# Five pieces of order and placement in a scan kernel: who scales the chunks, how diagonals are made, how scores alternate

## The chip, the cores and the metric

The kernel runs on one core of a Trainium2 chip. Its time is device microseconds of one launch; the median of several runs counts. A profile is one further execution, recorded by the hardware profiler. The engines are TensorE (PE: matmuls; PEld is its weight load), VectorE (DVE), ScalarE (ACT), GpSimd (POOL) and SyncE (SP, which here issues all DMAs).

## The reference, cut to what matters

Two layers over x (2 batches, 1024 tokens, 256 features). The first is a selective state-space layer with an MLP, run forward and backward in time; the second is attention with 16 heads of 16 and an MLP of 1024.

```python
def _ssm(h, in_w, xproj_w, dt_bias, A_log, Dskip, out_w):   # fwd, then bwd
    xz = h @ in_w
    xs, z = jnp.split(xz, 2, axis=-1)                       # 512 channels each
    xs = jax.nn.silu(xs)
    proj = xs @ xproj_w
    dt = jax.nn.softplus(proj[..., :D_INNER] + dt_bias)
    Bm = proj[..., D_INNER:D_INNER + D_STATE]               # 64 states
    Cm = proj[..., D_INNER + D_STATE:]
    A = -jnp.exp(A_log)
    def step(hst, ins):
        dt_t, B_t, C_t, x_t = ins
        dA = jnp.exp(dt_t[:, :, None] * A)
        hst = hst * dA + (dt_t * x_t)[:, :, None] * B_t[:, None, :]
        y_t = jnp.einsum('bds,bs->bd', hst, C_t)
        return (hst, y_t)
    ...
    return y * jax.nn.silu(z) @ out_w
# h is a layer norm of x times (1 + scale) plus shift, both from the condition vector
# attention: softmax(q k^T / 4, with a key mask) v, 16 heads; then an MLP
```

## The kernel before

**Units and steps.** Time is cut into two halves of 512 tokens. With 2 directions and 2 batches that makes 8 units, one after the other. A unit has 64 steps, one for each state of the 64. In a step every one of 512 channels (4 tiles f of 128 partitions) is scanned over 512 tokens for this state. The four engines form a pipeline:

- ScalarE makes `decay` = exp(dt x a) for each f (L1091) and, one step ahead, three of four token tiles of dt x x scaled by this state's B (`uT`, L1073).
- TensorE turns them to channels-on-partitions in PSUM (`turn_u`, L1652 and L1655). Of the four token tiles, three are plain transposes (L1655) and one (L1652) is a product with a diagonal matrix `diag` that holds B, which scales and turns at once. It then sums the products of step w - 2 over the states into four PSUM banks (`reduce_state`, L1661).
- VectorE scans (L1319), one instruction for each f.
- GpSimd multiplies the states by the row of C (L789), two f at a time.

Rings tie them: three PSUM banks for `turn_u` (TensorE can be three tiles ahead of the scan), three buffers of decay and uT (ScalarE up to three steps ahead), three of the states.

**Diagonals.** In the first unit ScalarE makes the diagonal tile of every step (L1076, in `scan_input`). For later units the diagonals lie in DRAM: SyncE fills a zeroed array (`fill_diag`, 16 fills for each of two arrays, one fill for each pair of steps of the first unit), stores B onto its diagonal (`store_diag`, 8 stores a unit) and loads two tiles for each pair of steps (`load_diag`). On the same queue it asks for the rows of C for each pair, first in each pair.

**Tiles between the steps.** All other matrix work of the layer is cut into tiles that have a fixed slot among the steps. `TURN[u]` (from `place_turns`, and `turns` for the last unit) says which tile TensorE begins at which step; each step gives it one piece (one matmul over 512 columns, or a group of transposes) after the second f. `act_turns` and `dve_turns` say what ScalarE and VectorE do after the scans of that step or one to six later: evict the tile, centre a chunk, take silu. Layer norm goes by chunks of 512 tokens: `mean` (TensorE), `centre` (VectorE), `square` (ScalarE, into `sq`), `sum` (TensorE), `std` (ScalarE, into `rstd`) and two steps after the sum `scale` (VectorE, L1183 and L1191: times rstd, then times scale plus shift, one tensor_scalar for each of two feature tiles). Inside the scan lie the scales of chunks 2 and 3 of `ln0` in the first unit, and chunks 0 to 2 of `ln1` in the last.

**Attention.** 16 blocks v of 16 m. For each m TensorE makes two scores that are exponentiated (`scores2`, three PSUM banks, freed by ScalarE's exp, L1116) and two first-pass scores of a later head (`scores`, L1712), whose maxima VectorE takes (L1382, four banks). After every second m come the products with v (`weigh_v`, L1739). 84 of the 512 first-pass scores are made before the blocks.

Of the kernel before, what the change touches and what calls it, by code (L numbers as in the profile page):

```python
# [54 lines left out]
SILU_STEP, LAST_SILU_STEP = 24, 18  # L55
# [5 lines left out]
DIAG_STORES = 8  # L61


def build(nc, t):
# [4 lines left out]
    with ctx:  # L69
# [79 lines left out]
        sq = {name: cut(at, 2, C, HALF) for name, (at, _) in NORM_AT.items()}  # L149
# [104 lines left out]
        def turns(u):  # L254

            yT_ = [("yT", u - 1, f) for f in range(NI)]
            zs_ = [("zs", u, c) for c in range(TB)]
            out_ = [("out", u - 1, c) for c in range(C)]
            return yT_ + zs_ + out_ + steps("mean", "ln1", 0, 1, 2) + steps("sum", "ln1", 0, 1, 2)\
                + up("ln1", 0, 0, 8)[::2] + up("ln1", 0, 0, 8)[1::2] + [("down", "ln1", 0, c) for c in range(C)]  # L260

        def place_turns(u):
# [18 lines left out]
            if u == 0:  # L281
                place(zs_[:2] + steps("mean", "ln0", 2, 3) + xs_[:2] + steps("sum", "ln0", 2, 3) + xs_[2:] + zs_[2:], 0)
# [43 lines left out]
        def dve_turns(u, st):  # L326
# [217 lines left out]
        def _(sp):  # L544
# [43 lines left out]

            def fill_diag(k):

                half, part = divmod(k, FILLS)
# [3 lines left out]
                dst = diag_dram[1 - half, part * n:(part + 1) * n].rearrange("n (k t) -> (n k) t", t=2 * P)\  # L595
                    .rearrange("(p r) t -> p r t", p=P)
                sp.dma_start(dst, zeros.unsqueeze(1).to_broadcast([P, n // 2, 2 * P]))                    .then_inc(s[f"diag_zero_{1 - half}"], 16)

            def store_diag(u, part):
# [3 lines left out]
                if u < 3 and part == 0:  # L603
                    sp.wait_ge(s[f"diag_zero_{u % 2}"], 16 * FILLS)
# [4 lines left out]
            def load_diag(p):  # L609

                u, pair = divmod(p, DS // 2)
                if u == 0 or u == UNITS:
                    return
                if pair == 0:
                    sp.wait_ge(s["diag_out"], 16 * DIAG_STORES * u)
                sp.wait_ge(s["u_full"], NI * 2 * (p - DIAG_PAIRS + 1))
                n = p - DS // 2
# [6 lines left out]
            for u in range(UNITS):  # L624
                sp.wait_ge(s["bc_out"], 16 * (u + 1))
                for pair in range(DS // 2):
# [7 lines left out]
                    if u == 0:  # L634
                        fill_diag(pair)
# [112 lines left out]
        def _(pool):  # L748
# [13 lines left out]

            def finish_dt(u, f):
# [11 lines left out]
            for u in range(UNITS):  # L775
                d, b, hi, half = unit(u)
                for st in range(DS):
# [60 lines left out]
        def _(act):  # L838
            def square(name, i):
# [9 lines left out]
                act.activation(sq[name][:, i % 2], src, ACT.Square).then_inc(s["squared"], 1)  # L849
# [215 lines left out]
            def scan_input(w, c):  # L1065
# [9 lines left out]
                elif u == 0:  # L1075
# [52 lines left out]
        def _(dve):  # L1128
# [64 lines left out]
            def copy_rows(u):  # L1193
# [3 lines left out]
                if u:  # L1197
                    dve.wait_ge(s["bc_out"], 16 * u)
                    dve.wait_ge(s["diag_out"], 16 * DIAG_STORES * (u - 1))
# [225 lines left out]
        def _(pe):  # L1425
# [17 lines left out]
            def mean_square(name, i):  # L1443
                pe.wait_ge(s["squared"], CHUNKS * NORMS.index(name) + i + 1)
                dst = take(pe, first["sum", name, i])
                yield from product(dst, [(mean_w[:, :], sq[name][:, i % 2, c]) for c in range(C)])
# [194 lines left out]
            def turn_u(w, f):  # L1641
# [3 lines left out]
                if f == 0:  # L1645
                    pe.wait_ge(s["uT_ready"], TB * (w + 1) - max(0, w + 1 - DS))
                if f == 0 and w % 2 == 0 and w >= DS:
                    pe.wait_ge(s[f"diag_in_{p % 2}"], 16 * ((p - DS // 2) // 2 + 1))
# [67 lines left out]
            def scores2(v, m):  # L1716
# [6 lines left out]
                for jj in range(2):  # L1723
                    j = 2 * pair + jj
                    n = 2 * w + jj
                    if n >= 3:
                        pe.wait_ge(s["probs_ready"], n - 2)
                    pe.matmul(psum[:, n % 3, :], stack[u % STACKS][0:ROWS, 1, j, kt * P:(kt + 1) * P],  # L1728
                              stack[u % STACKS][0:ROWS, 0, j, tok(qh)], start=True, stop=True)\
                      .then_inc(s["s2_full"], 1)  # L1730
# [77 lines left out]
```

## Time and profile before

| | us |
|---|---|
| runs, median (lowest, highest) | 3275.02 (3272.62, 3275.12) |
| the profiled execution's own time | 3272.75 |
| its span, first to last instruction | 3270.9 |
| TensorE busy, share of the span | 3194.7, 98% |
| VectorE busy | 2866.5, 88% |
| ScalarE busy | 2815.5, 86% |
| GpSimd busy | 2327.7, 71% |
| start of the scan's first unit, end of its last | 63.4, 2549.7 |
| attention blocks | 2710.6 to 3079.2 |

The profile's rows name engine, line and tiles. In a timeline a row is: start, length, engine, line, operation, tiles, count, and in brackets the idle time before it and what ended it. Rows of the same line that touch are merged, so that a row's length covers several instructions. `psum` and `arena` are the large tiles in which everything lies.

### The profile page before, as it was taken

What the parts mean: (1) busy time and instruction counts of PE and PEld (TensorE: products, weight loads), DVE (VectorE), ACT (ScalarE), POOL (GpSimd) and SP (SyncE); (2) the same over time, 40 slices, a digit from 0 to 9 for tenths busy, and PEclk for the clock granted to TensorE, in tenths of its full rate; (3) what the DMA queues carried; (4) which work ended last, traced back from release to release, by engine and by line L of the source; (5) the groups of instructions that cost most, each with busy time, mean ns of one, the idle gap of its engine ahead of it and who ended that gap; (6) DMA issues with size and microseconds to landing.
All of it is one profiled execution on the core that took longest, in us unless ns stands there. A gap on an engine that the chain in (4) does not pass through costs nothing.

```text
span 3270.9 us, 59384 instructions
## 1 busy us (share of the span) xinstructions
PE 3194.7 (98%) x22634; PEld 2505.6 (77%) x22634; DVE 2866.5 (88%) x2863; ACT 2815.5 (86%) x4659; POOL 2327.7 (71%) x1113
## 2 busy tenths in 40 slices
PE   8999999999999999999999999999999999999899
PEld 5888898999899998999998999999888542222244
DVE  3999999999999999999999999999999578888121
ACT  6999999999999999999999999999989436777620
POOL 1899999999999999999999999999878220000000
PEclk8999999999999999999999999999999999999999
DMA  3223222212222222222222222222212043422000
GB/s 121 69 84 81 80 72 69 72 67 72 69 73 93 70 70 75 72 69 72 73 73 74 67 72 67 74 68 71 86 57 69 29 102 59 77 34 31 15 7 20
DMA packets 199837, 218.82 MB, mean 67 GB/s; under 512 B 79969, under 2 KB 149601, under 8 KB 199297
## 3 DMA queue, kind: packets, MB, share of 16 engines
q1 hardware_dynamic: 199554, 215.02, 23.1%
q8 instruction: 180, 2.95, 0.4%
q14 instruction: 103, 0.84, 0.1%
HBM read 194.29 MB, written 18.19 MB: 65 GB/s over the span
## 4 chain that ended last, share of the span: by engine, by line
PE 76%; ACT 15%; DVE 6%; issue 3%; DMA 0%; POOL 0%; DVEq 0%; ACTq 0%; SPq 0%
PE psum L1661 21%; PE psum L1429 17%; PE psum L1655 16%; PE psum L1652 12%; ACT arena L1091 6%; ACT arena L1073 5%; PE psum L1739 4%; PE psum L1728 3%; DVE arena L1319 2%; PE psum L1712 2%; DVE row_max L1382 2%; PE psum L1681 1%; ACT arena L1116 1%; ACT arena L1076 0%; ACT arena L920 0%
## 5 line engine op out<-in xcount | busy, mean ns | idle before, releaser
L1319 DVE TENSOR_TENSOR_SCAN arena<-arena,psum 128x512 f32<-128x512 f32 x2048 | 2373.8, 1230 | 58.6 <-PE psum L1655 45.6
L789 POOL TENSOR_TENSOR arena<-arena 128x1024 f32<-128x1024 f32 x1024 | 2225.8, 2185 | 257.1 <-DVE arena L1319 233.5
L1091 ACT ACTIVATE arena<-arena,a_neg 128x512 f32<-128x512 f32 x2048 | 1442.9, 724 | 45.4 <-PE psum L1655 44.9
L1661 PE MATMUL psum<-ident,arena 128*128 128x128 f32 x8192 | 1231.9, 273 | 1.7 <-POOL arena L789 1.7
L1073 ACT ACTIVATE arena<-arena,bT 128x512 f32<-128x512 f32 x1536 | 1110.7, 723 | 0.0
L1655 PE MATMUL psum<-ident,arena 128*128 128x128 f32 x6144 | 1009.8, 273 | 0.0
L1661 PEld LDWEIGHTS psum<-ident,arena 128*128 128x128 f32 x8192 | 962.7, 141 | 2.1 <-POOL arena L789 2.1
L1652 PE MATMUL psum<-arena 128*128 128x128 f32 x4096 | 821.1, 282 | 31.8 <-ACT arena L1073 16.5
L1652 PEld LDWEIGHTS psum<-arena 128*128 128x128 f32 x4096 | 648.3, 191 | 246.6 <-issue 151.9
L1655 PEld LDWEIGHTS psum<-ident,arena 128*128 128x128 f32 x6144 | 744.2, 142 | 0.0
L1429 PE MATMUL psum<-arena 128*128 128x512 f32 (+1 forms) x1440 | 672.0, 587 | 5.2 <-DVE arena L1191 2.9
L1429 PEld LDWEIGHTS psum<-arena 128*128 128x128 f32 x1440 | 248.7, 192 | 172.4 <-issue 163.8
L1116 ACT ACTIVATE arena<-psum 128x512 f32<-128x512 f32 x512 | 267.2, 604 | 108.1 <-PE psum L1728 108.1
L1382 DVE TENSOR_REDUCE row_max<-psum 128x1 f32<-128x512 f32 x512 | 317.0, 682 | 44.8 <-PE psum L1712 44.1
L833 POOL TENSOR_TENSOR arena<-arena 128x512 f32<-128x512 f32 x8 | 10.2, 1274 | 385.5 <-DMA arena<-sums_dram 385.5
L1728 PEld LDWEIGHTS psum<-arena 100*128 100x128 bf16 x512 | 39.3, 97 | 179.1 <-ACT arena L1116 155.4
L1728 PE MATMUL psum<-arena 100*128 100x512 bf16 x512 | 160.4, 386 | 8.6 <-ACT arena L1116 6.6
L1712 PE MATMUL psum<-arena 97*128 97x512 bf16 x512 | 157.8, 386 | 6.6 <-DVE row_max L1382 6.6
L1739 PE MATMUL psum<-arena 128*32 128x512 f32 x1024 | 136.4, 604 | 4.6 <-ACT skip_w L1106 4.5
L1012 ACT ACTIVATE arena<-psum,b_up 128x512 f32<-128x512 f32 x32 | 22.0, 687 | 101.9 <-PE psum L1429 101.9
L1712 PEld LDWEIGHTS psum<-arena 97*128 97x128 bf16 x512 | 50.6, 99 | 67.9 <-DVE row_max L1382 22.3
L1233 DVE SCALAR_TENSOR_TENSOR arena<-psum,b_up,arena 128x512 f32<-128x512 f32 x32 | 24.0, 751 | 75.0 <-PE psum L1429 75.0
(118 smaller groups left out, 871.9 us busy)
## 6 DMA issues: line engine op xcount, KB each, us to landing
arena<-bc_dram SPq DMA_DIRECT2D x256, 512.0 KB, 3.7
arena<-diag_dram SPq DMA_DIRECT2D x224, 128.0 KB, 2.1
arena<-qk_dram SPq DMA_DIRECT2D x96, 128.0 KB
diag_dram<-arena SPq DMA_DIRECT2D x32, 256.0 KB, 4.4
qk_dram<-arena SPq DMA_DIRECT2D x8, 768.0 KB, 3.4
arena<-in_x SPq DMA_DIRECT2D x4, 512.0 KB, 10.5
arena<-skip_w SPq DMA_DIRECT2D x64, 32.0 KB, 2.0
arena<-sums_dram SPq DMA_DIRECT2D x64, 32.0 KB, 1.8
```

The source lines that it names most:

```text
L789: pool.tensor_tensor(out[:, :, way], h_now[:, :, way], c_row, ALU.mult)\
L1073: act.activation(uT[w % AHEAD][:, c - DIAGS], dtxT[:, u % 2, c], ACT.Copy, scale=bT[:, u % 2, c, st:st + 1])\
L1091: act.activation(decay[:, w % AHEAD, f], dt_[:, u % 2, f], ACT.Exp, scale=a_neg[:, d, f, st:st + 1])\
L1116: act.activation(probs[:, w % 4, jj], psum[:, n % 3, :], ACT.Exp)\
L1319: dve.tensor_tensor_scan(hs[:, w % RING, f, rows][:, way], decay[:, w % AHEAD, f, way], psum[:, 4 + n % U_BANKS, way], end_state(w - DS, f ...
L1382: dve.tensor_reduce(row_max[:, j, qt, kh:kh + 1], side_bank("scores", w), axis=AX.X, op=ALU.max)\
L1429: o = pe.matmul(dst, lhsT, rhs, start=k == 0, stop=k == len(pairs) - 1)
L1652: o = pe.matmul(dst[:, c * P:(c + 1) * P], dtxT[:, w // DS % 2, c, f * P:(f + 1) * P], diag[:, p % DIAG_PAIRS, w % 2], start=True, stop=True)
L1655: o = pe.transpose(dst[:, c * P:(c + 1) * P], uT[w % AHEAD][:, c - DIAGS, f * P:(f + 1) * P], ident[:, :])
L1661: return pe.matmul(psum[:, c, f * P:(f + 1) * P], hs[:, w % RING, f, at:at + P], ident[:, :], is_transpose=True, start=False, stop=w % DS ...
L1712: pe.matmul(take_side(pe, "scores", w), stack[u % STACKS][0:PLAIN, 0, j, qt * P:(qt + 1) * P], stack[u % STACKS][0:PLAIN, 1, j, tok(kh)], ...
L1728: pe.matmul(psum[:, n % 3, :], stack[u % STACKS][0:ROWS, 1, j, kt * P:(kt + 1) * P], stack[u % STACKS][0:ROWS, 0, j, tok(qh)], start=True, ...
```

## The change

Chunks inside the scan are scaled by GpSimd instead of VectorE, at the same step (two after the sum). The last unit's tiles stand in another order; its silu comes at step 23 instead of 18, and the squares of its chunks go to another place (that of `xs`, hence a new wait). In the first unit the chunks' means and sums are spread. Diagonals of the first unit's steps 32 to 63 come from DRAM: half of the second array is filled first, two fills for each of the first four pairs, then four stores are made in pairs 4 to 7; the other fills follow. In attention `scores2` makes one score at a time, and a first-pass score follows each.

```diff
-SILU_STEP, LAST_SILU_STEP = 24, 18
+SILU_STEP, LAST_SILU_STEP = 24, 23
...
+ACT_DIAGS = 32
...
-        sq = {name: cut(at, 2, C, HALF) for name, (at, _) in NORM_AT.items()}
+        def sq(name, i):
+            at = R_XS if name == "ln1" and i < CHUNKS - 1 else NORM_AT[name][0]
+            return cut(at + i % 2 * C * HALF, C, HALF)
...
-            return yT_ + zs_ + out_ + steps("mean", "ln1", 0, 1, 2) + steps("sum", "ln1", 0, 1, 2)\
-                + up("ln1", 0, 0, 8)[::2] + up("ln1", 0, 0, 8)[1::2] + [("down", "ln1", 0, c) for c in range(C)]
+            return steps("mean", "ln1", 0) + yT_ + zs_[:1] + steps("sum", "ln1", 0) + zs_[1:2] + steps("mean", "ln1", 1) + zs_[2:]\
+                + steps("sum", "ln1", 1) + out_ + steps("mean", "ln1", 2) + up("ln1", 0, 0, 8)[:4:2] + steps("sum", "ln1", 2)\
+                + up("ln1", 0, 0, 8)[4::2] + up("ln1", 0, 0, 8)[1::2] + [("down", "ln1", 0, c) for c in range(C)]
...
-                place(zs_[:2] + steps("mean", "ln0", 2, 3) + xs_[:2] + steps("sum", "ln0", 2, 3) + xs_[2:] + zs_[2:], 0)
+                place(zs_[:1] + steps("mean", "ln0", 2) + zs_[1:2] + xs_[:1] + steps("sum", "ln0", 2) + steps("mean", "ln0", 3)
+                      + xs_[1:3] + steps("sum", "ln0", 3) + xs_[3:] + zs_[2:], 0)
...
-            back = TURN[u].get(st - 2)
-            if back and back[0] == "sum":
-                todo += steps("scale", *back[1:])
...
+            late_fills = ACT_DIAGS * FILLS // DS
+            FILL_ORDER = [(0, k) for k in range(late_fills, FILLS)] + [(1, k) for k in range(FILLS)] + [(0, k) for k in range(late_fills)]
+            first_stores = DIAG_STORES * (DS - ACT_DIAGS) // DS
+            def fill_at(k):
+                if k < FILLS - late_fills:
+                    return k // 2
+                k -= FILLS - late_fills
+                return 4 + (k * 3 // 4 if k < FILLS else k)
...
-                if u < 3 and part == 0:
-                    sp.wait_ge(s[f"diag_zero_{u % 2}"], 16 * FILLS)
+                if u < 3 and part == (0 if u else DIAG_STORES - first_stores):
+                    sp.wait_ge(s[f"diag_zero_{u % 2}"], 16 * (FILLS if u else FILLS - late_fills))
...
-                if u == 0 or u == UNITS:
+                n = p - ACT_DIAGS // 2
+                if n < 0 or u == UNITS:
                     return
...
                     if u == 0:
-                        fill_diag(pair)
+                        for k in range(2 * FILLS):
+                            if pair == fill_at(k):
+                                fill_diag(k)
+                        if 0 <= pair - FILLS // 4 < first_stores:
+                            store_diag(0, DIAG_STORES - first_stores + pair - FILLS // 4)
...
+            def scale(name, i):
+                k = NORMS.index(name)
+                n = CHUNKS * k + i
+                b, half = chunk(name, i)
+                out = h[:, :, b, tok(half)]
+                pool.wait_ge(s["rstd_ready"], n + 1)
+                pool.tensor_tensor(out, out, rstd[name][:, i].unsqueeze(1).to_broadcast([P, C, HALF]), ALU.mult)\
+                    .then_inc(s["normed"], 1)
+                pool.wait_ge(s["normed"], n + 1)
+                for c in range(C):
+                    pool.tensor_scalar(out[:, c], out[:, c], mods[:, k, C + c, b:b + 1], mods[:, k, c, b:b + 1], ALU.mult, ALU.add)\
+                        .then_inc(s["h_ready"], 1)
...
+                    back = TURN[u].get(st - 2)
+                    if back and back[0] == "sum":
+                        scale(*back[1:])
...
+                if (name, i) == ("ln1", 0):
+                    act.wait_ge(s["reduce_done"], NI * ((UNITS - 1) * DS + 1))
...
-                elif u == 0:
+                elif w < ACT_DIAGS:
                     act.activation(diag[:, w // 2 % DIAG_PAIRS, w % 2], ident[:, :], ACT.Copy, scale=bT[:, 0, c, st:st + 1])\
                        .then_inc(s["uT_ready"], 1)
...
-                if f == 0 and w % 2 == 0 and w >= DS:
-                    pe.wait_ge(s[f"diag_in_{p % 2}"], 16 * ((p - DS // 2) // 2 + 1))
+                if f == 0 and w % 2 == 0 and w >= ACT_DIAGS:
+                    pe.wait_ge(s[f"diag_in_{p % 2}"], 16 * ((p - ACT_DIAGS // 2) // 2 + 1))
...
-            def scores2(v, m):
+            def scores2(v, m, jj):
...
-                    scores2(v, m)
-                    for w in scores_at(v, m):
-                        scores(w)
+                    others = list(scores_at(v, m))
+                    for jj in range(2):
+                        scores2(v, m, jj)
+                        for w in others[jj:jj + 1]:
+                            scores(w)
```

## Rows read from the trace of the kernel before

**Rows 1.** The stretches' table: us, then each engine's busy us, granted clock, DMA.

```profile
core 0: us, PE busy (x) PEld busy (x) DVE busy (x) ACT busy (x) POOL busy (x), PEclk, DMA share, GB/s
231.74:388.25 156.51, 147.22 (x1196) 134.10 (x1195) 146.63 (x129) 156.51 (x275) 148.67 (x73) 1.00 0.29 83
848.75:999.54 150.79, 150.79 (x1219) 137.80 (x1218) 145.74 (x131) 148.92 (x247) 148.16 (x74) 1.00 0.28 83
2221.92:2549.71 327.79, 316.70 (x2459) 283.77 (x2458) 324.81 (x284) 294.67 (x467) 279.89 (x129) 0.98 0.20 67
2404.00:2409.00 5.00, 5.00 (x26) 5.00 (x25) 4.33 (x5) 4.06 (x7) 4.17 (x2) 0.50 0.09 26
```

**Rows 2.** The chain of waits, first unit's second half, shares by line.

```profile
by line: ACT arena L1091 47.4%; ACT arena L1073 36.6%; ACT arena L1076 5.4%; issue 1.7%; ACT arena L888 1.5%; ACT arena L889 1.5%; ACT arena L903 1.3%; ACT arena L899 1.3%; ACT arena L928 1.2%; PE psum L1655 0.8%; PE psum L1661 0.8%; PE psu
```

**Rows 3.** VectorE's timeline in the third unit, and in the last.

```profile
870.18 4.55 DVE L1319 TENSOR_TENSOR_SCAN arena<-arena,psum 128x512 f32<-128x512 f32 x4 [0.25 <-PE psum L1655]
...
943.73 46.75 DVE L1319 TENSOR_TENSOR_SCAN arena<-arena,psum 128x512 f32<-128x512 f32 x42
...
2242.18 52.99 DVE L1319 TENSOR_TENSOR_SCAN arena<-arena,psum 128x512 f32<-128x512 f32 x45
```

**Rows 4.** ScalarE's timeline, step starts in the first unit and the third.

```profile
229.80 0.73 ACT L1091 ACTIVATE arena<-arena,a_neg 128x512 f32<-128x512 f32 x1
...
234.39 0.74 ACT L1091 ACTIVATE arena<-arena,a_neg 128x512 f32<-128x512 f32 x1
...
968.87 1.35 ACT L1091 ACTIVATE arena<-arena,a_neg 128x512 f32<-128x512 f32 x2
...
973.16 1.36 ACT L1091 ACTIVATE arena<-arena,a_neg 128x512 f32<-128x512 f32 x2
```

**Rows 5.** Groups by line, ScalarE in the first unit.

```profile
L1076 ACT ACTIVATE arena<-ident,bT 128x128 f32<-128x128 f32 x62 | 25.7, 415 | 5.9 <-PE psum L1655 5.9
```

**Rows 6.** DMA issues: KB each, median us to landing.

```profile
arena<-diag_dram SPq DMA_DIRECT2D x224, 128.0 KB, 2.1
...
diag_dram<-arena SPq DMA_DIRECT2D x32, 256.0 KB, 4.4
```

**Rows 7.** VectorE's timeline around the last unit's second and third scale.

```profile
2398.28 1.19 DVE L1183 TENSOR_TENSOR arena<-arena 128x1024 f32<-128x1024 f32 x1
2399.50 2.72 DVE L1191 TENSOR_SCALAR arena<-arena,mods 128x512 f32<-128x512 f32 x2
...
2408.88 1.28 DVE L1319 TENSOR_TENSOR_SCAN arena<-arena,psum 128x512 f32<-128x512 f32 x1 [0.64 <-PE psum L1655]
2411.21 2.45 DVE L1319 TENSOR_TENSOR_SCAN arena<-arena,psum 128x512 f32<-128x512 f32 x2 [1.05 <-PE psum L1655]
...
2425.36 3.62 DVE L1319 TENSOR_TENSOR_SCAN arena<-arena,psum 128x512 f32<-128x512 f32 x3 [0.58 <-PE psum L1655]
```

**Rows 8.** Groups by line: busy us, mean ns of one, idle before.

```profile
L766 POOL TENSOR_TENSOR arena<-arena 128x512 f32<-128x512 f32 x28 | 35.8, 1280 | 0.0
...
L1191 DVE TENSOR_SCALAR arena<-arena,cmod 128x512 f32<-128x512 f32 x16 | 8.0, 543 | 0.3
```

**Rows 9.** Timeline of a fed step: GpSimd's product, TensorE that reads it.

```profile
2378.13 2.18 POOL L789 TENSOR_TENSOR arena<-arena 128x1024 f32<-128x1024 f32 x1 [0.17 <-DVE arena L1319]
...
2383.23 0.60 PE L1661 MATMUL psum<-ident,arena 128*128 128x128 f32 x4
...
2383.89 0.49 PE L1655 MATMUL psum<-ident,arena 128*128 128x128 f32 x3
```

**Rows 10.** Timeline of two m in attention.

```profile
2825.13 0.60 PE L1728 MATMUL psum<-arena 100*128 100x512 bf16 x2
...
2825.62 2.07 ACT L1116 ACTIVATE arena<-psum 128x512 f32<-128x512 f32 x4 [0.83 <-PE psum L1728]
...
2826.01 0.65 PE L1728 MATMUL psum<-arena 100*128 100x512 bf16 x2
...
2828.02 0.60 PE L1728 MATMUL psum<-arena 100*128 100x512 bf16 x2
```

More of the change, by code:

```diff
@@ L587, in store_c @@
                 sp.dma_start(bc_dram[u], bc_rows[DS:2 * DS, :]).then_inc(s["bc_out"], 16)
+            late_fills = ACT_DIAGS * FILLS // DS
[6 more added lines that the diff above has]
+                return 4 + (k * 3 // 4 if k < FILLS else k)
             def fill_diag(k):
-                half, part = divmod(k, FILLS)
                 if k == 0:
@@ L594, in fill_diag @@
                 n = DS // FILLS
-                dst = diag_dram[1 - half, part * n:(part + 1) * n].rearrange("n (k t) -> (n k) t", t=2 * P)\
+                which, part = FILL_ORDER[k]
+                dst = diag_dram[which, part * n:(part + 1) * n].rearrange("n (k t) -> (n k) t", t=2 * P)\
                     .rearrange("(p r) t -> p r t", p=P)
-                sp.dma_start(dst, zeros.unsqueeze(1).to_broadcast([P, n // 2, 2 * P]))                    .then_inc(s[f"diag_zero_{1 - half}"], 16)
+                sp.dma_start(dst, zeros.unsqueeze(1).to_broadcast([P, n // 2, 2 * P]))                    .then_inc(s[f"diag_zero_{which}"], 16)
             def store_diag(u, part):
@@ L611, in load_diag @@
                 u, pair = divmod(p, DS // 2)
-                if u == 0 or u == UNITS:
+                n = p - ACT_DIAGS // 2
+                if n < 0 or u == UNITS:
                     return
-                if pair == 0:
-                    sp.wait_ge(s["diag_out"], 16 * DIAG_STORES * u)
+                if n == 0 or pair == 0:
+                    sp.wait_ge(s["diag_out"], 16 * (first_stores + DIAG_STORES * u))
                 sp.wait_ge(s["u_full"], NI * 2 * (p - DIAG_PAIRS + 1))
-                n = p - DS // 2
                 if n >= 2:
@@ L848, in square @@
                 src = (h if name.startswith("ln") else x)[:, :, b, tok(half)]
-                act.activation(sq[name][:, i % 2], src, ACT.Square).then_inc(s["squared"], 1)
+                act.activation(sq(name, i), src, ACT.Square).then_inc(s["squared"], 1)
             def std(name, i):
@@ L1198, in copy_rows @@
                     dve.wait_ge(s["bc_out"], 16 * u)
-                    dve.wait_ge(s["diag_out"], 16 * DIAG_STORES * (u - 1))
+                    dve.wait_ge(s["diag_out"], 16 * DIAG_STORES * (u - 1) + 16 * DIAG_STORES * (DS - ACT_DIAGS) // DS)
                 dve.tensor_copy(bc_rows[:, :], bank(g)).then_inc(s["bc_rows_ready"], 1)
@@ L1445, in mean_square @@
                 dst = take(pe, first["sum", name, i])
-                yield from product(dst, [(mean_w[:, :], sq[name][:, i % 2, c]) for c in range(C)])
+                yield from product(dst, [(mean_w[:, :], sq(name, i)[:, c]) for c in range(C)])
             def h_ready(name, i):
@@ L1722, in scores2 @@
                     pe.wait_ge(s["rows_in"], 16 * PARTS * (u + 1))
[L1723 to L1730, printed above, removed]
+                j = 2 * pair + jj
+                n = 2 * w + jj
+                if n >= 3:
+                    pe.wait_ge(s["probs_ready"], n - 2)
+                pe.matmul(psum[:, n % 3, :], stack[u % STACKS][0:ROWS, 1, j, kt * P:(kt + 1) * P],
+                          stack[u % STACKS][0:ROWS, 0, j, tok(qh)], start=True, stop=True)\
+                  .then_inc(s["s2_full"], 1)
             def weigh_v(v, kt):
```

2 lines of the change are left out of this document (1 added, 1 removed).

## The prediction

> **What bounds the kernel now.** I read the stretches first, then the chain, then single engines. The page's first part has TensorE busy nearly throughout, but that is a mean over stages with different limits. The table of stretches splits the scan [rows 1]. The second half of the first unit (32 steps) takes 156.5 us, with ScalarE busy for all 156.51 of it and TensorE for 147.2. The same half of the third unit has the same scan and the same kinds of tiles, and takes 150.8 us with TensorE busy throughout. So the first unit is held by ScalarE and the later ones by TensorE. The chain of waits says the same of that half: three ScalarE lines, L1091, L1073 and L1076, are 89% of it [rows 2]. L1076 is the instruction that makes a diagonal tile.
>
> The last unit takes 327.8 us with VectorE busy for 324.8 [rows 1]. It is bound by VectorE, which does its 256 scans and all that lies between them.
>
> Three rates are used below. When VectorE is fed, a backward step (4 scans) takes 52.99 x 4 / 45 = 4.71 us, a forward one 46.75 x 4 / 42 = 4.45. When TensorE must add a tile's piece to each step, the step is 4.55 + 0.25 = 4.80 us, the 0.25 being a wait for TensorE; there are 8 such steps on end [rows 3].
>
> **The change part by part.**
>
> *Diagonals of the first unit.* ScalarE starts a step every 234.39 - 229.80 = 4.59 us where it makes one diagonal, and every 973.16 - 968.87 = 4.29 us where it makes none (the second stretch holds no other work) [rows 4]. So one diagonal costs 0.29 to 0.30 us of ScalarE's pace; the 415 ns that its row shows overlap the neighbours [rows 5]. The 32 that go are worth 32 x 0.295 = 9.4 us of ScalarE. What is late next is TensorE at 4.80 per step while tiles are interleaved, and VectorE at 4.45 afterwards. The third unit shows that mix, two output tiles included that the first has not: 150.8. I expect 150, thus 6.5 us won of the 9.4, with 5.7 (156.5 - 150.8) as the low end and 9.4 as the high one. SyncE gets 16 more loads of 128 KB (2.1 us from issue to landing, against some 9.6 us that two steps leave) and 4 small stores, and issues two fills at a time in the first four pairs. The store's wait for the fills stands one pair behind the last of them, and a fill lands 4.4 us after its issue [rows 6]. GpSimd's rows of C are asked for ahead of all these in each pair. I cost it at nothing; a late C row would show as GpSimd waiting for a DMA.
>
> *Chunk scaling from VectorE to GpSimd, twice in the first unit and three times in the last.* On VectorE one takes 1.20 for the product and 2.72 for the two tensor_scalar: 3.9 us until the next scan [rows 7]. The tensor_scalar of the same shape takes 0.54 late in the kernel, where GpSimd is idle [rows 8]; here the first stands until GpSimd's product has ended. Between the second and the third VectorE waited 0.64 + 1.05 us for TensorE, and 0.58 after the third [rows 7]. In that stretch, 2404 to 2409, the granted clock was 0.50, the level of 1.2 GHz, and TensorE had idled during the scaling before [rows 1]. So the last unit loses 3 x 3.9 + 2.3 = 14.0 us.
>
> In the first unit two such holds cost VectorE 7.8 us, but ScalarE, which sets the end there, stood idle for only 5.9 in all, every bit of it waiting for TensorE behind those holds [rows 5]. I take 5.9 for this half; the 2 us that are left are VectorE's new reserve.
>
> What GpSimd pays: it already works 2.18 us per product, two products a step, with idle gaps of some 0.2 [rows 9]. The first operation of a scale is a product of the same size, 2.18. A tensor_scalar of 128x512 is in no row of GpSimd. From below: VectorE's 0.54. From above: a GpSimd sum of two operands of that shape, 1.28 [rows 8], and, further off, one of twice the size, 2.18. I take 1.28, the same engine and shape. A scale is then 2.18 + 2 x 1.28 = 4.7 us (3.3 to 6.5), and the next state product is late by that less 0.2, by 4.5 us.
> The Trainium skill, GPSIMD Engine Reference, section 4.1 (Engine selection), speaks against the change: keep elementwise work on VectorE, GpSimd being about 2x slower with two inputs and near line rate with one. The trace agrees on the first part (2.18 for GpSimd's product of 1024 elements a partition, 1.20 for VectorE's). By that page's best loop (769 ns for 512 elements, section 3.1) a scale would be an estimated 3.7 us and the last unit's loss below would be nil.
>
> Who waits for that: TensorE reads the product that ended at 2380.31 only from 2383.23, 2.9 us later [rows 9]. VectorE then has one scan running and two more tiles ready, between 2.4 and 3.5 us of work at 1.18 a scan, and TensorE's next tile is done 1.15 us after that read (2383.89 + 0.49). That leaves 1.2 to 2.4 more, and I take 1.8. So 4.7 us are free against 4.5. GpSimd catches up by little: two products back to back, with 0.1 between, need 2 x 2.28 of a step's 4.71, 0.15 us a step, and all that VectorE does besides scans (a centring 1.2, an output 0.7). In the new order the last unit's scales come after steps 14, 24 and 40. Between the first two about 3 us are made good, so the second is over by some 1.5 us; before the third all of it is. I book 1.5, with 0 (short form) and 7 (long form) as ends. In the first unit it hides behind the 2 us of reserve and a TensorE that runs less far ahead. VectorE's waits ended by TensorE, TensorE's by GpSimd, is what is late next.
>
> *New order of the last unit's tiles.* The same 21 tiles in the same 56 slots, centrings and outputs at other steps. The silu of the gates goes from step 18 to 23, where ScalarE is again several us ahead. The first square now waits for the first reduction, which is five steps old. With the holds gone TensorE has fewer pauses in which to catch up: up to five more steps at 4.80 in place of 4.71, 0.5 us. Sum of the last unit: 14.0 - 1.5 - 0.5 = 12.0 us.
>
> *Scores one by one.* Per two m TensorE runs 4 second scores, 4 first-pass scores and 8 products with v, in 2828.02 - 2825.13 = 2.89 us. The pair at 2825.13 shows 0.60, that at 2826.01 shows 0.65 [rows 10]: its second matmul waits for the exp that frees its bank. That exp can start only at 2825.62 and needs 0.6. With first-pass scores between, the fourth second score comes at 1.3 us instead of 1.1 and no longer waits. That is 0.05 us per two m, and there are (512 - 84) / 4 = 107 such groups: 4.9 us. VectorE's reduces get their scores evenly, and 4 x 0.6 = 2.4 us of them fit in 2.84. From both sides: a gain of nothing if another wait takes its place, 8 us if it also eases the stalls at the block ends; a loss of 3 if the alternation holds a score back.
>
> **The sum.** 6.5 + 5.9 + 12.0 + 4.9 = 29.3 us off the profiled execution's 3272.75 gives 3243.5. That execution stands 2.3 us below the median of the runs (3275.02), and with the median it is 3245.7. I say 3244.5. I count as no change what lies within 0.2%, 6.5 us, about what a measurement of this kernel can tell.
>
> **The rivals.**
> A. The alternation is worth nothing, since TensorE has no other idle time in the group: 3244.5 + 4.9 = 3249.5. For it: only 0.05 us of waiting in 2.89. Chance 0.12.
> B. GpSimd's tensor_scalar is dear (2.2 us or more). The scale takes 6.5 us, overruns by 1.7, 3.5 and 1.7 in the last unit, and TensorE's pauses bring the half clock back once, 2.3 us as before: 3244.5 + 7.7 = 3252. If it takes 3 us, all five overrun and the moved work gains next to nothing; only the diagonals and the scores stay (11.4): 3275 - 11.4 = 3263.6. Chances 0.12 and 0.06. Against it: the product of two operands costs 1.28.
> C. More is won: a cheap tensor_scalar (no overrun, 1.5), all 9.4 us of ScalarE and the eased block ends (3): 3244.5 - 7.4 = 3237. Chance 0.12.
> D. Slower: GpSimd becomes the bound. A scale of D us costs the scan D - 4.9 each time, less the 2 us of reserve. It eats the whole gain where 5 x (D - 4.9) - 2 exceeds 29.3, at D = 11.2, a tensor_scalar of 4.5 us. At 6 us each (D = 14.2) it is 3244.5 - 1.5 + 44.5 = 3287.5. For it: the form is in no row of GpSimd, and a row of C late on SyncE's queue would add to it. Against: 3.5 times its dearest row of that shape. Chance 0.05.
> E. The first unit stays where it is because something else (GpSimd's products, or TensorE with its half clock early on) sets its pace: 3244.5 + 12.4 = 3257. Chance 0.05.
>
> **The numbers.** My forecast has 0.48 and its own range of 3240 to 3249. The range for 8 in 10 takes in A, C and the first part of B: 3235 to 3256. Faster by over 0.2% (below 3268.5): all but D and part of the dear end of B, 0.92. Within 0.2%: 0.03. Slower: 0.05.
>
> **What would show it.** The first unit's second half near 150 us with ScalarE no longer full, L1076 with 32 instructions, and ScalarE's 5.9 us of waiting gone. The last unit near 316 us, no VectorE row of 2.7 us for the scaling, no stretch at half clock in it, and TensorE waiting for GpSimd's product once, by a few us. A GpSimd tensor_scalar row of 0.8 to 1.3 us. Groups of two m at 2.84 us. Wrong would be: a GpSimd row above 2.2 us, VectorE idle behind TensorE after steps 14, 24 or 40, GpSimd waiting for C, or groups at 2.89 or more.

## The result, and the profile after

The changed kernel takes 3247.64 us (median; 3244.18 to 3249.24) against 3273.82 (3272.40 to 3275.12) of the kernel before on the same chip, a ratio of 0.9917 (95% interval 0.9904 to 0.993). That is 26.2 us less. The forecast was 29.3 by its parts, and 30.5 from the median of 3275.02 to the 3244.5 that it named. A second comparison (the changed kernel beside the combined version, below) gave 0.9913 (0.9898 to 0.9928). The profiled execution took 3246.55 us, its span is 3244.7. VectorE's busy time fell by 21.2 us, ScalarE's by 9.6, and GpSimd's rose by 11.2.

The table of stretches, with the columns of [rows 1], now for the first unit's two halves, the last unit, and a stretch at half clock:

```profile
65.17:230.03 164.86, 158.71 (x1223) 141.86 (x1222) 148.44 (x134) 164.26 (x279) 144.25 (x69) 0.98 0.29 84
230.03:378.05 148.02, 145.08 (x1199) 134.12 (x1198) 144.19 (x130) 145.13 (x240) 145.50 (x72) 1.00 0.30 86
2211.98:2527.69 315.71, 310.79 (x2459) 279.02 (x2458) 313.12 (x275) 294.25 (x466) 287.26 (x137) 1.00 0.21 70
196.20:203.00 6.80, 5.68 (x24) 4.76 (x23) 4.92 (x5) 6.80 (x12) 4.47 (x3) 0.50 0.16 51
```

Set against before, by the same marks (start of the first scan of the stretch to the start of the next stretch's; the last unit to the end of its last scan):

| stretch | before, us | after, us | difference | forecast |
|---|---|---|---|---|
| ahead of the first scan | 63.4 | 65.2 | +1.7 | 0 |
| first unit, steps 0 to 31 | 168.3 | 164.9 | -3.4 | -5.9 |
| first unit, steps 32 to 63 | 156.5 | 148.0 | -8.5 | -6.5 |
| six middle units | 1833.7 | 1833.9 | +0.2 | 0 |
| last unit | 327.7 | 315.7 | -12.1 | -12.0 |
| between scan and attention blocks | 161.0 | 160.9 | -0.1 | 0 |
| attention blocks | 368.6 | 364.1 | -4.5 | -4.9 |
| end | 191.7 | 192.1 | +0.4 | 0 |

Each part came in the stretch where it was expected. In size the last unit and attention agree, while the first unit's halves missed by 2.5 us (too little won) and 2.0 us (more won).

In the first unit's second half ScalarE is no longer full (145.1 of 148.0, against 156.51 of 156.51 in [rows 1]). Two things hold it now, one after the other. For 14 steps TensorE adds a tile's piece to each, and VectorE waits 0.25 us for it in each, 4.81 us a step. From 310.93 on VectorE scans for 67.2 us without a pause:

```profile
294.73 4.55 DVE L1359 TENSOR_TENSOR_SCAN arena<-arena,psum 128x512 f32<-128x512 f32 x4 [0.25 <-PE psum L1695]
...
310.93 67.20 DVE L1359 TENSOR_TENSOR_SCAN arena<-arena,psum 128x512 f32<-128x512 f32 x60 [0.17 <-ACT arena L1131]
```

That is 67.20 x 4 / 60 = 4.48 us a step, near the forecast's 4.45 for a fed VectorE. GpSimd runs without a pause in that time too, and the chain of waits (shares by line, as in [rows 2]) passes through its products; which of the two would have to become faster first, no run shows.

```profile
by line: POOL arena L824 56.9%; PE psum L1701 9.5%; issue 8.8%; PE psum L1695 7.4%; PE psum L1469 5.3%; PE psum L1692 5.0%; POOL arena L808 3.4%; POOL arena L801 2.6%; DVE arena L1359 1.5%; DVEq L1357 0.0%
```

The scaling on GpSimd. First the timeline of one scale in the last unit (start, length, engine, line, ..., count), then the group of its tensor_scalar (busy us, mean ns of one, idle before):

```profile
2288.44 2.38 POOL L791 TENSOR_TENSOR arena<-arena 128x1024 f32<-128x1024 f32 x1
2290.93 1.52 POOL L795 TENSOR_SCALAR arena<-arena,mods 128x512 f32<-128x512 f32 x2
2292.41 6.43 POOL L824 TENSOR_TENSOR arena<-arena 128x1024 f32<-128x1024 f32 x3
```

```profile
L795 POOL TENSOR_SCALAR arena<-arena,mods 128x512 f32<-128x512 f32 x10 | 7.6, 769 | 0.5
```

The scale's product takes 2.38 us, a tensor_scalar 0.77, and from the scale's start to the next state product pass 2292.41 - 2288.44 = 3.97 us. The forecast had 4.7 from two ends, 3.3 and 6.5. Its sentence on the Trainium skill (GPSIMD Engine Reference, section 3.1) had an estimate of 3.7 for the whole and 769 ns for the tensor_scalar; the row of 769 ns agrees.

Two things were not foreseen. The first is in the last unit: TensorE idles before the output tile of step 24. TensorE's row, and ScalarE's around it:

```profile
2332.84 1.10 PE L1469 MATMUL psum<-arena 128*128 128x512 f32 x2 [1.83 <-ACT arena L900]
```

```profile
2323.20 1.28 ACT L960 ACT_TABLE_LOAD   x1
2324.49 1.92 ACT L960 ACTIVATE arena<-arena 128x2048 f32<-128x2048 f32 x1
2326.43 1.28 ACT L1137 ACT_TABLE_LOAD   x1
...
2332.03 0.66 ACT L900 ACTIVATE arena<-psum,eps 128x512 f32<-128x512 f32 x1
```

Silu and two table loads hold ScalarE for 4.5 us at step 23. The sum's eviction (L900) comes behind them and the exponentials and scaled tiles of one more step, at 2332.03. The tiles between the steps share one PSUM bank, so TensorE cannot begin the next tile before, and waits 1.83 us.

The second is in the first unit. TensorE idles behind the silu burst of step 24, and its granted clock falls to 0.50 (1.2 GHz) just after, the stretch 196.2 to 203.0 of the first table. VectorE waited 3.30 us for ScalarE there. The kernel before has the same burst, with one pause of 1.41 us and full clock. The rows are TensorE's before, TensorE's after (two), VectorE's after:

```profile
202.16 0.49 PE L1652 MATMUL psum<-arena 128*128 128x128 f32 x2 [1.41 <-ACT arena L1073]
```

```profile
195.37 0.49 PE L1692 MATMUL psum<-arena 128*128 128x128 f32 x2 [2.29 <-DVE arena L1359]
...
198.03 0.80 PE L1692 MATMUL psum<-arena 128*128 128x128 f32 x2 [1.12 <-ACT arena L1113]
```

```profile
194.10 4.58 DVE L1359 TENSOR_TENSOR_SCAN arena<-arena,psum 128x512 f32<-128x512 f32 x4 [3.30 <-ACT arena L1131]
```

By the starts of the steps' first scans, counted from the unit's first, the changed kernel was 8.1 us ahead of the kernel before when step 24 began, and 3.5 when step 27 began. What VectorE's two holds had cost was won, and over half of it was given back at the burst.

In attention, first- and second-pass scores now alternate every 0.22 us, and the group of two m takes 2813.29 - 2810.45 = 2.84 us against 2.89 [rows 10]:

```profile
2810.45 0.39 PE L1767 MATMUL psum<-arena 100*128 100x512 bf16 x1
2810.67 0.38 PE L1752 MATMUL psum<-arena 97*128 97x512 bf16 x1
...
2813.29 0.39 PE L1767 MATMUL psum<-arena 100*128 100x512 bf16 x1
```

### The profile page after: what moved, and what is told of

It reads as the page before. It is cut to its first block, busy times and chain, and to the rows that moved or that the text cites. A ratio compares the mean times of both kernels' runs of the same rounds, so it can differ in the third digit from the quotient of the medians.

```text
span 3244.7 us, 59428 instructions
## 1 busy us (share of the span) xinstructions
PE 3181.8 (98%) x22634; PEld 2506.4 (77%) x22634; DVE 2845.3 (88%) x2848; ACT 2805.9 (86%) x4627; POOL 2338.9 (72%) x1128
## 4 chain that ended last, share of the span: by engine, by line
PE 72%; ACT 16%; DVE 5%; issue 4%; POOL 3%; DMA 0%; DVEq 0%; ACTq 0%; SPq 0%
PE psum L1701 19%; PE psum L1469 16%; PE psum L1695 14%; PE psum L1692 11%; ACT arena L1131 7%; ACT arena L1113 5%; PE psum L1778 4%; PE psum L1767 3%; DVE arena L1359 3%; POOL arena L824 3%; PE psum L1752 3%; DVE row_max L1422 1%; PE psum L1721 1%; ACT arena L1156 1%; ACT arena L960 0%
## 5 line engine op out<-in xcount | busy, mean ns | idle before, releaser
L1767 PE MATMUL psum<-arena 100*128 100x512 bf16 x512 | 189.9, 384 | 8.6 <-ACT arena L1156 6.6
L1752 PE MATMUL psum<-arena 97*128 97x512 bf16 x512 | 191.9, 387 | 5.3 <-DVE row_max L1422 5.3
L1767 PEld LDWEIGHTS psum<-arena 100*128 100x128 bf16 x512 | 48.2, 97 | 169.1 <-ACT arena L1156 132.5
```

The source lines that it names most:

```text
L1752: pe.matmul(take_side(pe, "scores", w), stack[u % STACKS][0:PLAIN, 0, j, qt * P:(qt + 1) * P], stack[u % STACKS][0:PLAIN, 1, j, tok(kh)], ...
```

## The experiments

All lengths of stretches below are by the marks of the table above, from the profile of each kernel. Except in the comparison marked below, a kernel was timed once. Ahead of the first scan, where nothing differs, these times vary by 4.5 us (last section), so the stretches carry the argument and not the whole times.

**Scaling back on VectorE.**

```diff
 # dve_turns
+            back = TURN[u].get(st - 2)
+            if back and back[0] == "sum":
+                todo += steps("scale", *back[1:])
 # GpSimd's loop
-                    if back and back[0] == "sum":
-                        scale(*back[1:])
```

> The changed kernel, with the scaling of chunks inside the scan back on VectorE at the same steps; the new order, the diagonals and the scores stay. Theory (the holds of VectorE were the loss): the last unit goes from 315.7 us back to 326 to 330 (three holds of 3.9, and up to 2.3 if the pauses of TensorE bring its half clock back), VectorE rows of 2.7 us for the two tensor_scalar reappear five times, the first unit goes from 312.9 to 316 to 319 (ScalarE idles again behind the two holds); in all 14 to 20 us, 3261 to 3267. Rival (the new order of the last unit's tiles won the time): the last unit stays at or below 318 us and the whole within 6 us of 3247.

Measured: 3259.93 us. The last unit takes 326.9 us, 11.2 more than in the changed kernel, which is three holds of 3.9 less a bit; a short spell of half clock came with it.

```profile
2213.47:2540.32 326.85, 313.63 (x2459) 280.59 (x2457) 324.00 (x284) 294.87 (x466) 279.81 (x128) 0.99 0.20 67
```

```profile
L1231 DVE TENSOR_SCALAR arena<-arena,mods 128x512 f32<-128x512 f32 x6 | 8.2, 1401 | 0.1
```

The six tensor_scalar average 1.40 us where they run beside GpSimd's products (0.54 in [rows 8]). With the new order and no move the last unit is only 0.8 us shorter than before (326.9 against 327.7), so the order alone, its silu at step 23 included, won next to nothing. But the move alone does not give 12.1 us either, only 6.8 (the scaling alone, below): it needs the new order, which sets the scales further apart.

The first unit grew by only 1.5 us, less than the 3 to 6 expected, and so the whole is 1 us below the expected range. When step 24 began it was 6.2 us behind the changed kernel, but it made good 4.7 of them at the burst, where its pause was the short one of 1.41 us and the clock stayed full.

**All diagonals by ScalarE.**

```diff
-ACT_DIAGS = 32
+ACT_DIAGS = 64
```

with the fills one for each pair.

> The changed kernel, with all 64 diagonals of the first unit made by ScalarE (the fills then go one for each pair of steps, no loads in the first unit). Theory (ScalarE's 0.295 us for each diagonal set the pace of the second half): its 32 steps go from 148.0 us back to 156 to 158, ScalarE full again, the first half stays within 1 us; in all 8.5 to 9.5 us more, 3255 to 3258. Rival (the move of the scaling, or the clock, made that half quicker): it stays below 151 us.

Measured: 3257.49 us. The second half takes 155.9 us, 7.9 more, with ScalarE at 154.3:

```profile
231.93:387.81 155.88, 146.66 (x1196) 134.04 (x1195) 146.43 (x129) 154.29 (x271) 148.59 (x73) 1.00 0.30 83
```

The theory holds; the size is a hair below its range. 32 diagonals are worth 7.9 us there, not the full 32 x 0.295, since at 148 the half is held by TensorE and then by VectorE and GpSimd. The other 0.6 us of that half's 8.5 is assigned to no part.

**Scores in pairs.**

```diff
-                    others = list(scores_at(v, m))
                     for jj in range(2):
                         scores2(v, m, jj)
-                        for w in others[jj:jj + 1]:
-                            scores(w)
+                    for w in scores_at(v, m):
+                        scores(w)
```

> The changed kernel, with the attention order of before: two second scores, then two first-pass scores. Theory (the fourth second score waited for its bank): a group of two m goes from 2.846 back to 2.89 us and the 16 blocks from 364.1 to 368 to 369 us, in all 4 to 5 us more. Rival (the blocks became shorter by another way, such as the stalls at block ends): the groups' median stays at 2.85 and only the blocks' ends differ.

Measured: 3251.05 us, the blocks 368.8 us against 364.1. A group is 2833.13 - 2830.24 = 2.89 us again, and the second pair of second scores shows 0.65 again:

```profile
2830.24 0.60 PE L1767 MATMUL psum<-arena 100*128 100x512 bf16 x2
...
2831.12 0.65 PE L1767 MATMUL psum<-arena 100*128 100x512 bf16 x2
...
2833.13 0.60 PE L1767 MATMUL psum<-arena 100*128 100x512 bf16 x2
```

**The scaling alone**, put into the kernel before.

> The kernel before, with nothing changed but the scaling moved to GpSimd. A scale there is 2.18 + 2 x 0.77 = 3.7 us, and in this order the last unit has three of them after steps 32, 34 and 36. Theory (2.9 us until TensorE reads a product and 1.8 of tiles ready for VectorE are free, and little is caught up in two steps): the first costs nothing, the second some 2.2 us, the third some 3.3, so the last unit takes 313.7 + 5.5 = 319 us (317 to 321). Rival 1 (only the 2.9 are free): 321 to 323. Rival 2 (GpSimd's lateness is hidden wholly): 314. The first unit: 324.8 less 5.9 of ScalarE's idle time, plus up to 2.4 if the silu burst brings the half clock, 319 to 322. In all 3258 to 3262.

Measured: 3265.80 us; first half 162.2, last unit 320.9. In the last unit the first of the three scales (at 2385.26) cost nothing: VectorE scans on until 2403.31. After the second and the third TensorE waited over 2 us for GpSimd's product, and VectorE behind it:

```profile
67.54:229.73 162.19, 157.32 (x1223) 140.53 (x1222) 148.46 (x134) 161.62 (x276) 144.42 (x69) 0.99 0.24 75
2219.84:2540.71 320.87, 312.83 (x2459) 280.37 (x2458) 313.53 (x275) 294.54 (x467) 287.92 (x137) 0.99 0.20 69
```

```profile
2403.89 0.66 PE L1676 MATMUL psum<-ident,arena 128*128 128x128 f32 x4 [2.36 <-POOL arena L801]
...
2416.35 0.88 PE L1676 MATMUL psum<-ident,arena 128*128 128x128 f32 x4 [2.62 <-POOL arena L801]
```

```profile
2384.12 19.19 DVE L1334 TENSOR_TENSOR_SCAN arena<-arena,psum 128x512 f32<-128x512 f32 x16
...
2418.43 1.28 DVE L1334 TENSOR_TENSOR_SCAN arena<-arena,psum 128x512 f32<-128x512 f32 x1 [2.91 <-PE psum L1670]
2421.20 9.60 DVE L1334 TENSOR_TENSOR_SCAN arena<-arena,psum 128x512 f32<-128x512 f32 x8 [1.50 <-PE psum L1670]
```

The first unit's half is 6.1 us shorter than before, as the forecast's 5.9 had it. In the last unit 7.2 us were lost, 2.7 and 4.5, where 2.2 and 3.3 were expected. The total of 320.9 does not tell the theory (317 to 321) from the rival in which only TensorE's 2.9 us are free (321 to 323). The row of the first scale does: it held GpSimd for 3.96 us, 0.9 more than 2.9 and the gap of 0.2 together, and VectorE did not wait. Of the third scale's 4.5 us the second wait, 1.50, came in a spell of half clock (2416.6 to 2420.1). The whole lies above the expected range, as 4.1 us of it fall ahead of the first scan, where nothing was changed.

**The last unit's silu after step 26.**

```diff
-SILU_STEP, LAST_SILU_STEP = 24, 23
+SILU_STEP, LAST_SILU_STEP = 24, 26
```

> The changed kernel, with the last unit's silu of the gates after step 26 instead of 23. Theory: in the changed kernel TensorE idles 1.83 us at step 24, since its output tile needs the one bank that the sum's tile holds until ScalarE, busy with table loads and silu, evicts it. After step 26 stand output tiles, which VectorE evicts, so that pause goes: step 24 falls from 6.9 to 4.8 us and the last unit from 315.7 to 313.6 (313 to 314.2), 2 us in all. Rival (ScalarE's work as such is late there, and the pause only moves): the last unit stays at 315 to 316.

Measured: 3248.43 us in all, of which 2.7 more than in the changed kernel's profile lie ahead of the first scan. The last unit takes 313.6, 2.1 less, and the whole difference is in step 24 (6.88 us in the changed kernel, 4.80 now):

```profile
2214.71:2528.29 313.58, 310.51 (x2459) 278.91 (x2457) 313.13 (x275) 293.92 (x466) 287.33 (x137) 1.00 0.21 70
```

**Sixteen diagonals by ScalarE.**

```diff
-ACT_DIAGS = 32
+ACT_DIAGS = 16
...
-                    return k // 2
+                    return k // 3
...
-                        if 0 <= pair - FILLS // 4 < first_stores:
-                            store_diag(0, DIAG_STORES - first_stores + pair - FILLS // 4)
+                        for k in range(first_stores):
+                            if pair == FILLS // 4 + k // 2:
+                                store_diag(0, DIAG_STORES - first_stores + k)
```

> The changed kernel, with only 16 of the first unit's diagonals by ScalarE (fills three for each pair, six stores in pairs 4 to 6, loads from pair 8 on). Theory (ScalarE sets the first half as well, and TensorE's pause behind the silu burst brings the half clock): by step 24 ScalarE is 9 x 0.295 = 2.7 us earlier, the pause of 2.3 + 1.1 us shrinks, no half clock near 196 us, and the first half goes from 164.9 to 160 us (159 to 161.5), the second stays at 148. Rival 1 (the half clock stays): 162 to 163. Rival 2 (TensorE or GpSimd bound that half, not ScalarE): 164 to 165. Should SyncE's waits hold back rows of C, GpSimd shows waits for DMA and the half gets longer.

Measured: 3243.72 us. The first half takes 158.9 us, 6.0 less, a little better than 159, and there is no half clock near 196. All but 0.7 us of it is won in steps 24 to 26. Its chain of waits up to the silu burst is TensorE's now:

```profile
67.84:226.69 158.85, 156.55 (x1223) 140.47 (x1222) 148.31 (x133) 158.25 (x261) 144.18 (x69) 0.99 0.33 97
226.69:374.75 148.06, 145.10 (x1199) 134.13 (x1198) 144.25 (x130) 146.14 (x242) 145.45 (x72) 1.00 0.28 79
```

```profile
by line: PE psum L1702 27.2%; PE psum L1696 22.6%; PE psum L1470 16.2%; PE psum L1693 15.9%; DVE arena L1360 7.0%; PE psum L1722 2.9%; issue 2.7%; DVE arena L1204 2.0%; ACT arena L961 1.5%; ACT L1138 1.0%; ACT arena L1132 0.6%; ACT arena L1
```

**A scale nearly twice as long.** After the two tensor_scalar on GpSimd:

```diff
-                        .then_inc(s["h_ready"], 1)
+                        .then_inc(s["again"], 1)
+                scales = (0, 0, 0, 1)[i] if name == "ln0" else 2 + i
+                for r in range(2):
+                    pool.wait_ge(s["again"], C * (2 * scales + r + 1))
+                    for c in range(C):
+                        pool.tensor_scalar(out[:, c], out[:, c], 1.0, 0.0, ALU.mult, ALU.add)\
+                            .then_inc(s["h_ready" if r else "again"], 1)
```

> The changed kernel, with each scale followed by four more tensor_scalar of the same shape on GpSimd (times 1, plus 0), so that it holds GpSimd 2.18 + 6 x 0.77 + waits = 7.0 us instead of 3.7. Theory (2.9 us until TensorE reads, and 1.8 of tiles ready, are free; 3 us caught up in ten steps): the scan loses 2.1, 3.8 and 2.1 us at the last unit's three scales, so the last unit takes 315.7 + 8.0 = 324 us, up to 328 if TensorE's pauses bring the half clock. Rival 1 (only the 2.9 are free): 13.4 us more, 329 or above. Rival 2 (GpSimd is behind anyway and is caught up by what VectorE does besides): below 320. First half of the first unit: 165 to 169.

Measured: 3260.35 us, the last unit 327.3 us, 11.6 more; the first half 165.0. A scale held GpSimd for 6.6 us (the added ones took 0.6 each), not 7.0. The waits of TensorE in the last unit (who waited for whom: us in total, times, longest):

```profile
2213.76:2541.05 327.29, 316.42 (x2459) 282.57 (x2457) 313.46 (x275) 294.68 (x466) 294.94 (x149) 0.98 0.21 67
```

```profile
PE psum L1707 <- POOL arena L830: 6.0, 3, 2.0
```

```profile
2300.76 1.28 DVE L1365 TENSOR_TENSOR_SCAN arena<-arena,psum 128x512 f32<-128x512 f32 x1 [2.01 <-PE psum L1701]
2303.88 2.45 DVE L1365 TENSOR_TENSOR_SCAN arena<-arena,psum 128x512 f32<-128x512 f32 x2 [1.84 <-PE psum L1701]
```

TensorE waited three times, 2.0 us each, and each was followed by 3.4 us at half clock. So 3.97 us of scale cost nothing and 6.6 cost 3.9 each: of these, VectorE's first wait of 2.01 us is the lateness, and the second, 1.84, comes at half clock. The time of 327.3 lies in the theory's 324 to 328, but does not by itself exclude the rival with only 2.9 us free: its 13.4 us were for a hold of 7.0, and with 6.6 it would have 3 x 0.4 less, 327.9. VectorE's first wait decides. The product was 6.6 - 0.2 = 6.4 us late and VectorE stood 2.0, so 4.4 us were free, against the forecast's 4.7 and the rival's 2.9. The three waits are also equal (1.96 to 2.05), so ten steps were enough to make good what was left of the lateness, where the theory let the second scale cost 1.7 us more.

**The first unit's tiles in the old order.**

```diff
-                place(zs_[:1] + steps("mean", "ln0", 2) + zs_[1:2] + xs_[:1] + steps("sum", "ln0", 2) + steps("mean", "ln0", 3)
-                      + xs_[1:3] + steps("sum", "ln0", 3) + xs_[3:] + zs_[2:], 0)
+                place(zs_[:2] + steps("mean", "ln0", 2, 3) + xs_[:2] + steps("sum", "ln0", 2, 3) + xs_[2:] + zs_[2:], 0)
```

> The changed kernel, with the first unit's tiles in the old order (scales after steps 14 and 16 instead of 10 and 18). Theory (TensorE, less held up before step 24, runs further ahead, idles longer during the silu burst and falls to the half clock; ScalarE sets the time of step 25 either way): as in the kernel with the scaling alone, the pause is 1.4 us, no half clock near 196 us, the first half takes 162.2 to 162.6 instead of 164.9, 2.5 us less in all. Rival (the half clock there is a matter of where the runs happen to fall): it appears again and the half takes 164 to 165.

Measured: 3246.54 us. The first half takes 162.3 us, 2.5 less than in the new order, there is no half clock in it, and the pause behind the burst is 1.41 us, once. The rows are the stretch, TensorE's pause, and VectorE's first scan behind the burst:

```profile
66.49:228.82 162.33, 157.45 (x1223) 140.61 (x1222) 148.46 (x133) 161.75 (x275) 144.46 (x69) 0.99 0.29 85
```

```profile
199.24 0.49 PE L1691 MATMUL psum<-arena 128*128 128x128 f32 x2 [1.41 <-ACT arena L1112]
```

```profile
195.30 4.58 DVE L1358 TENSOR_TENSOR_SCAN arena<-arena,psum 128x512 f32<-128x512 f32 x4 [1.33 <-ACT arena L1130]
```

Behind the burst both kernels scan again at the same time after their first scan: 195.30 - 66.49 = 128.8 us here, 194.10 - 65.17 = 128.9 in the changed kernel. ScalarE sets that time. The changed kernel had come to it 1.9 us earlier, waited 3.30 us instead of 1.33, and lost its 2.5 us only afterwards, while its clock was at half.

**Both remedies, and the changed kernel beside it** (16 diagonals by ScalarE, silu after step 26). These two were timed four times each.

> The changed kernel with both remedies: 16 diagonals by ScalarE, and the last unit's silu after step 26. Theory: they act in different units and add up: first unit's first half 159 us instead of 164.9, last unit 313.6 instead of 315.7, so 8 us under the changed kernel, 3238 to 3241, with all else equal; what lies before the scan's start varies by some 4 us from run to run. Rival (the gains overlap, or later stretches take them back): 3242 or above.

> The changed kernel itself, timed beside the combined version on the same chip. 3245 to 3249 us, first half 164.9 with the half clock near 196 to 199 us, last unit 315.65.

Measured: 3239.70 us (3238.90 to 3240.45), ratio to before 0.9891 (0.9874 to 0.9907); the changed kernel 3247.62 (3244.30 to 3249.16), ratio 0.9913 (0.9898 to 0.9928). The difference of 7.9 us is about the sum of both remedies (6.0 and 2.1), as expected; the changed kernel's own half and unit are again 164.8 and 315.6 us. This is the fastest version.

```profile
65.15:224.17 159.02, 155.52 (x1223) 139.52 (x1222) 148.32 (x133) 158.42 (x261) 144.35 (x69) 1.00 0.33 97
2206.18:2519.75 313.57, 310.50 (x2459) 278.93 (x2457) 313.12 (x275) 293.93 (x467) 287.41 (x137) 1.00 0.21 70
```

**The combined version with the old order in the first unit.**

> The combined version with the first unit's tiles in the old order, scales after steps 14 and 16. Theory (two scales two steps apart overrun what is free, as in the last unit of the kernel with the scaling alone, and ScalarE no longer hides it): the second holds the scan 2.5 us or so, of which TensorE's pieces and ScalarE's burst hide a part: the first half is 0.5 to 3 us above 159. Rival (ScalarE still hides it wholly): 158.5 to 159.3.

Measured: 3244.97 us; the first half takes 161.5, 2.5 more, and TensorE waits 2.2 us for GpSimd there:

```profile
67.84:229.31 161.47, 155.67 (x1223) 139.49 (x1222) 148.42 (x133) 159.00 (x262) 144.47 (x69) 1.00 0.33 96
```

```profile
PE psum L1701 <- POOL arena L824: 2.2, 1, 2.2
```

So the new order of the first unit's tiles loses 2.5 us with 32 diagonals on ScalarE and wins 2.5 with 16. With 32 the old order's wait for GpSimd (1.83 us of TensorE's time) was hidden behind ScalarE's burst; with 16 it is not.

## Why the prediction was right, point by point

- **Two kinds of bound (right).** ScalarE in the first unit and VectorE in the last. Giving either its work back brings time back there: 7.9 us for the diagonals, 11.2 for the three scales.
- **Diagonals, 6.5 us (8.5: too small, within its bounds of 5.7 and 9.4).** What is late next was named rightly, TensorE at 4.80 us a step and then VectorE at 4.45; mis-sized was the allowance for two output tiles that the third unit has and the first has not. I allowed 0.8 us for them. Step by step the two halves agree within 0.3 us but where those tiles stand, and the whole difference is 150.8 - 148.0 = 2.8 us. Left out of the list was GpSimd, which runs without a pause in the last 105 us of that half.
- **Scaling in the first unit, 5.9 us (3.4).** ScalarE's idle time did go (0.5 us of the 5.9 is left), and 6.1 us are won in the kernel with the scaling alone and 6.0 with the old order. The term failed by 2.5 us, because the silu burst, which the trace of before shows with a pause of 1.4 us behind it, now found TensorE and VectorE further ahead. The pauses grew to 2.29 + 1.12 us and half clock followed. I had used the half clock only as something that the change takes away.
- **GpSimd's price (right, with the nearest row a bit dear).** 3.97 us from scale to product against 4.7. In the last unit TensorE waited for GpSimd 0.4 us in all, as much as before, so the booked overrun of 1.5 us was 0. The free lateness, put at 4.7 us, measures 4.4.
- **The last unit, 12.0 us (12.1, by luck: the errors cancel).** With the silu after step 26 the unit is 327.7 - 313.6 = 14.1 us shorter than before, all of the 14.0 that the forecast had as the cost of the holds. So neither the booked overrun of 1.5 nor the 0.5 for steps at TensorE's pace was paid. The silu at step 23, costed at nothing because ScalarE is "several us ahead", cost 2.1: being ahead hides the exponentials, but not the eviction that stands behind the burst in ScalarE's order and frees the only bank. The run with the silu after step 26 shows it.
- **Scores, 4.9 us (4.5), right.** The mechanism is the 0.05 us wait; the pairs bring it back. (107 x 0.05 is 5.4, not the 4.9 that the forecast wrote; 4.5 is 0.042 a group.)
- **The sum.** With the start 1.7 us later, not forecast and not the change's, and 0.5 elsewhere, the profile's 26.2 us is complete. The first unit's two misses, 2.5 and 2.0 us, have opposite signs, so the sum is closer than its parts. The range of 3235 to 3256 was wide enough; my own narrower one, 3240 to 3249, too. Of the rivals A, B and D fell by their rows: the scores moved, a tensor_scalar took 0.77 us, and GpSimd was not the bound of the last unit. C had two of its three pieces right (no overrun, and 8.5 of ScalarE's 9.4 us), but the block ends did not ease. Rival E had one grain of truth, the half clock in the first unit.

## What to carry to other kernels

Ask of an engine that runs ahead not only how far ahead it is, but what stands behind its longest instruction in its own order and who needs that: here an eviction that frees the single bank. When a stall is taken away, look at every known burst downstream, since an engine that is no longer held back meets it earlier and pauses longer. A pause of TensorE can cost about twice its length if half clock follows (2.0 us cost 3.9 with the heavy scale). An unknown price on an engine is best bounded by how late its result may come, and that can be read beforehand: the time from the end of a product to the read of it (2.9 us here), and what the engines behind it still have ready (1.5 us more). Moved work also wants room: the same three scales cost 7.2 us two steps apart and nothing ten or more apart.

## What the runs showed of the hardware

- Ahead of the first scan the instructions are the same in all profiles, yet that stretch took 63.4 to 67.9 us. The rows are those of the kernel before and of the old-order run, with a mean granted clock of 0.90 and 0.85. The clock is not the cause, since the longest, 67.9 us, had 0.96; what is stays open:

```profile
0.00:63.43 63.43, 48.81 (x163) 26.32 (x164) 14.66 (x30) 32.76 (x54) 1.65 (x12) 0.90 0.46 143
```

```profile
0.00:66.49 66.49, 51.92 (x163) 29.07 (x164) 14.66 (x29) 32.93 (x54) 1.65 (x12) 0.85 0.47 145
```

With a spread of 4.5 us there and one of 2.5 us (159.7 to 162.2) between scan and attention, one time of one run cannot tell the parts of this change; the last unit of the scan repeats within 0.1 us (315.63 to 315.66 in six profiles).
- TensorE's granted clock fell to 0.50 for 6.8 us after pauses of 2.29 and 1.12 us with 1.5 us of work between, and for 3.4 us after each of three single pauses of 2.0 in the last unit. It stayed at 1.00 after a single 1.41 or 1.83, but also after single pauses of 2.55 (kernel before, at 2390.2), 2.68 and 2.54 (scaling back on VectorE, at 170.7 and 2292.9), 2.36 (scaling alone, at 2403.9) and 2.23 (combined version with the old order, at 166.2). So the length of a pause alone does not tell what the clock will do.
- A tensor_scalar of 128x512 float32 with two scalars from SBUF took 0.77 us on GpSimd, with immediate scalars 0.6 (the heavy scale); on VectorE 0.54 alone, and 1.4 on average beside GpSimd's products (scaling back on VectorE).
- Between silu and exponentials ScalarE loaded a table in 1.28 us and went on at once: load, silu of 2048 elements a partition and load were 4.5 us.
